# Input-gate block products of a GRU loop in four 32-column groups, spread over all steps

## What is computed

```python
def cell(h, x):
    gi = x @ W_ih + b_ih
    gh = h @ W_hh + b_hh
    i_r, i_z, i_n = jnp.split(gi, 3, axis=-1)
    h_r, h_z, h_n = jnp.split(gh, 3, axis=-1)
    r = jax.nn.sigmoid(i_r + h_r)
    z = jax.nn.sigmoid(i_z + h_z)
    n = jnp.tanh(i_n + r * h_n)
    h_new = (1.0 - z) * n + z * h
    return (h_new, h_new)
```

## Time and profile before

| | us |
|---|---|
| median of three runs | 2352.3 (2351.1 to 2355.22) |
| the profiled execution, its own time | 2354.45 |
| its span, first to last instruction | 2352.6 |
| TensorE matmul busy | 2237.2 (95%) |
| TensorE weight load busy | 1678.7 (71%) |
| VectorE busy | 1406.8 (60%) |
| ScalarE busy | 1184.1 (50%) |
| GpSimd busy | 1141.6 (49%) |
| instructions | 172984 |

### The profile page before, as it was taken

The page is one execution under the profiler, slowest core; times in us unless marked ns, Lnnn a source line. Parts: engine busy times, 40 slices in busy tenths (PEclk is TensorE's granted clock), DMA queues, the critical chain, the costliest instruction groups (busy, mean ns, idle before and its releaser), DMA issues.

```text
span 2352.6 us, 172984 instructions
## 1 busy us (share of the span) xinstructions
PE 2237.2 (95%) x69632; PEld 1678.7 (71%) x69632; DVE 1406.8 (60%) x5056; ACT 1184.1 (50%) x5995; POOL 1141.6 (49%) x3895
## 2 busy tenths in 40 slices
PE   6899999997889999999999999999999999999998
PEld 2223333332369999888999988899998888888887
DVE  1433434343246666677666667766666677777776
ACT  2344444443035555555555555555555555555565
POOL 1142334223125555566555555655555566666665
PEclk8899999998899999999999999999999999999999
DMA  5000000001100000000000000000000000000001
GB/s 232 1 1 1 1 1 1 1 5 50 47 21 15 15 14 8 7 6 7 15 14 17 10 6 5 7 15 14 15 12 6 8 4 7 5 4 7 4 7 71
DMA packets 30281, 40.50 MB, mean 17 GB/s; under 512 B 3296, under 2 KB 24032, under 8 KB 29408
## 3 DMA queue, kind: packets, MB, share of 16 engines
q1 hardware_dynamic: 30032, 36.87, 5.4%
q10 hardware_dynamic: 144, 2.10, 0.2%
HBM read 26.37 MB, written 12.58 MB: 17 GB/s over the span
## 4 chain that ended last, share of the span: by engine, by line
PE 65%; DVE 5%; issue 1%; DMA 0%; ACT 0%; SPq 0%; ACTq 0%
PE ps L1012 57%; PE ps L1038 5%; DVE arena L851 4%; PE ps L1048 3%; DVE arena L868 1%; DMA out<-arena 0%; DMA arena<-gi_d 0%; DVE arena L932 0%; SPq L799 0%; ACT ps L944 0%; SPq L806 0%; ACT arena L997 0%; ACT arena L975 0%; ACT ps L948 0%; ACT arena L980 0%
## 5 line engine op out<-in xcount | busy, mean ns | idle before, releaser
L1012 PE MATMUL ps<-whh,arena 128*4 128x128 f32 (+1 forms) x65536 | 1453.6, 246 | 52.4 <-DVE arena L868 43.6
L1012 PEld LDWEIGHTS ps<-whh,arena 128*4 128x4 f32 x65536 | 1320.0, 87 | 167.9 <-DVE arena L868 84.4
L851 DVE STREAM_TRANSPOSE arena<-ps 128x128 f32<-128x128 f32 x1024 | 432.1, 422 | 260.9 <-PE ps L1012 260.7
L969 ACT ACTIVATE arena<-arena 128x8 f32<-128x8 f32 x1024 | 216.4, 211 | 738.5 <-DVE arena L851 736.8
L1098 POOL TENSOR_TENSOR arena<-tap,seq 128x32 f32<-128x32 f32 x1024 | 231.7, 258 | 368.3 <-DVE seq L881 368.3
L320 DVE TENSOR_REDUCE top<-ps 128x2 f32<-128x1024 f32 x128 | 150.8, 1220 | 281.8 <-PE ps L516 281.8
L868 DVE TENSOR_TENSOR_SCAN arena<-arena 128x24 f32<-128x24 f32 x1024 | 217.2, 212 | 145.5 <-ACT arena L980 145.5
L944 ACT ACTIVATE ps<-arena 128x128 f32<-128x128 f32 x1026 | 269.9, 263 | 3.4 <-DMA arena<-gi_d 3.4
L857 DVE STREAM_TRANSPOSE arena<-ps 128x64 f32<-128x64 f32 x1024 | 256.9, 251 | 16.2 <-PE ps L1012 5.7
L1098 POOL TENSOR_TENSOR arena<-tap,arena 128x32 f32<-128x32 f32 x1024 | 231.6, 257 | 66.8 <-POOL arena L1108 66.8
L170 POOL TENSOR_TENSOR arena<-arena 128x2048 f32<-128x2048 f32 x16 | 72.3, 4520 | 350.0 <-ACT arena L244 350.0
(11 more groups left out here) (94 smaller groups left out, 1573.0 us busy)
## 6 DMA issues: line engine op xcount, KB each, us to landing
arena<-gi_d SPq DMA_DIRECT2D x256, 32.0 KB
gi_d<-arena SPq DMA_DIRECT2D x96, 64.0 KB, 1.6
seq<-in_x SPq DMA_DIRECT2D x4, 1024.0 KB, 16.8
out<-arena SPq DMA_DIRECT2D x16, 256.0 KB, 3.1
whh<-in_w_hh SPq DMA_DIRECT2D x1, 3072.0 KB, 20.1
arena<-in_w_emb ACTq DMA_DIRECT2D x1, 2048.0 KB, 8.2
arena<-in_w_qk SPq DMA_DIRECT2D x4, 512.0 KB, 12.0
arena<-in_w_rz SPq DMA_DIRECT2D x1, 2048.0 KB, 7.6
```

The source lines that it names most:

```text
L851: e.transpose(trn[:, h].rearrange("p q (i c s) -> p q c i s", c=2, s=2)[:, :, :, :, 0], bank[RN[h]][:, 0:P].rearrange("p (q c i) -> p q c ...
L969: e.activation(r_d0[:, h].rearrange("p (i s) -> p i s", s=2)[:, :, 1], trn[:, h, 0, 0:2 * NH].rearrange("p (i s) -> p i s", s=2)[:, :, 0], ...
L1012: last = e.matmul(bank[dst[h]][32 * G:32 * G + B, 0:n], hv, wv[:, k, gates, G, 64 * h:64 * h + 64], start=False, stop=k2 == 1 and k == C - ...
```

## The change

The blocks are made in another form, at other places, and from other loops.

- Form: each 128 x 128 product is made as four products of 32 columns, one to each group of 32 PSUM partitions, as the step's own products are. Blocks alternate between two PSUM banks, 4 and 5.
- Place: the work is cut into chunks of one contraction step (four products: eight matmuls and eight loads). A "turn" is 32 steps and makes the 12 blocks (48 chunks) of one batch and one tile. `spread` deals them out: one chunk in mid step, ahead of the wait for the second half of the state, in 30 of 32 steps, and one more at the end of the step in 18 of 32. Twelve turns make all 144 blocks, over the first 384 steps.
- Operands: the 128 columns of x that a turn needs are first copied into `xb` (two buffers) by a DMA of SyncE's queue.
- Loops: TensorE's code is a loop of 6 iterations whose body has two turns written out, that is 64 steps, and then the old two-step loop for the last 128 steps. VectorE's is three loops of 4 iterations with 32 steps in the body. SyncE's is written out in full. ScalarE's and GpSimd's are as before.

```diff
@@ shared
+        xb = tile([P, 2, C, P])
-        RN, RZ, FB = (0, 1), (2, 3), 4
+        RN, RZ, FB = (0, 1), (2, 3), (4, 5)
+        TURN, NRZ = P // B, 2 * NG
+        BLOCKS = NRZ + C
+        TURNS = (TB - 1) * B
+        def spread():
+            left = [(i, k) for i in range(BLOCKS) for k in range(C)]
+            plan = []
+            for v in range(TURN):
+                mid = [left.pop(0)] if left else []
+                end = [left.pop(0)] if left and (v % 2 == 0 or v % 8 == 7) else []
+                plan.append((mid, end, [i for i, k in mid + end if k == C - 1]))
...
@@ sync
+                def bring_x(m):
+                    src = seq_cb[:, :, m % B, PAD + P * (m // B + 1):PAD + P * (m // B + 2)]
+                    e.dma_start(xb[:, m % 2], src).then_inc(s_xb[m % 2], 16)
...
+                for m in range(TURNS):
+                    for js in (range(0, 2), range(2, 4), range(4, NRZ), range(0)):
+                        for j in js:
+                            keep(m, j)
...
+                        next_half(first)
+                        first += HALF
+                    if m + 2 < TURNS:
+                        e.wait_ge(st["s_block"], BLOCKS * (m + 1))
+                        bring_x(m + 2)
@@ vector
+                for tile_ in range(TB - 1):
+                    with e.Fori(0, B) as b:
+                        m = e.snap(b + B * tile_)
+                        for v, (_, _, whole) in enumerate(plan):
+                            step(b * TURN + (P * tile_ + v), v % 2)
+                            for i in whole:
+                                if i < NRZ:
+                                    take_rz(m, i)
+                                else:
+                                    take_n(m, i, b, P * (tile_ + 1))
@@ tensor
                     e.wait_ge(st["s_seed_rn"], half[1])
                     products(RN, rn, 1, 0)
+                    mid()
                     e.wait_ge(st["s_h"], half[1])
...
                     products(RZ, z, 1, 1).then_inc(st["s_z"], 1)
+                    end()
+                def part(m, par, parts):
+                    for i, k in parts:
+                        if i == 0 and k == 0:
+                            e.wait_ge(s_xb[par], e.snap(m * 8 + (16 - 8 * par)))
+                        if k == 0:
+                            e.wait_ge(st["s_taken"], e.snap(m * BLOCKS + i + 1))
+                        for g in range(NG):
+                            q = slice(32 * g, 32 * g + 32)
+                            if i < NRZ:
+                                w, v = xb[:, par, k, q], wrz[:, k, P * i:P * i + P]
+                            else:
+                                c = i - NRZ
+                                w, v = wn[:, k, P * c + 32 * g:P * c + 32 * g + 32], xb[:, par, k, :]
+                            last = e.matmul(bank[FB[i % 2]][q, 0:P], w, v, start=k == 0, stop=k == C - 1)
+                        if k == C - 1:
+                            last.then_inc(st["s_block"], 1)
...
+                with e.Fori(0, TURNS // 2) as it:
+                    for par in range(2):
+                        m = e.snap(it * 2 + par)
+                        for v, (mid, end, _) in enumerate(plan):
+                            step(m * TURN + v, v % 2, lambda: part(m, par, mid), lambda: part(m, par, end))
+                with e.Fori(0, P // 2) as it:
+                    for v in range(2):
+                        step(it * 2 + (T - P + v), v, lambda: None, lambda: None)
```

More of the change, by code:

```diff
@@ L759, in build @@
         s_kept = [sem("s_kept0"), sem("s_kept1")]
-        RN, RZ, FB = (0, 1), (2, 3), 4
+        s_xb = [sem("s_xb0"), sem("s_xb1")]
+        RN, RZ, FB = (0, 1), (2, 3), (4, 5)
         N_CLEAR = 9
-        TILE_BLOCKS = B * 2 * NG + C * B
+        TURN, NRZ = P // B, 2 * NG
[8 more added lines that the diff above has]
+                plan.append((mid, end, [i for i, k in mid + end if k == C - 1]))
+            assert not left and not plan[-1][2]
+            return plan
+        plan = spread()
         def h_of(u, h):
@@ L812, in _, with keep, next_half @@
             def _(e):
[L813 to L818, removed]
+                def bring_x(m):
+                    src = seq_cb[:, :, m % B, PAD + P * (m // B + 1):PAD + P * (m // B + 2)]
+                    e.dma_start(xb[:, m % 2], src).then_inc(s_xb[m % 2], 16)
+                def keep(m, j):
+                    e.wait_ge(st["s_taken"], 2 + BLOCKS * m + j + 1)
+                    e.dma_start(gi_d[m % B, P * (m // B + 1):P * (m // B + 2), j, :], blk[:, j % 2]).then_inc(s_kept[j % 2], 16)
+                def next_half(first):
+                    e.wait_ge(st["s_seed_z"], 2 * (first - HALF))
+                    load_ring(e, first // HALF % 2, first)
                 for half in range(2):
@@ L823, in _ @@
                     e.sem_inc(s_kept[i], 16)
[L824 to L837, removed]
+                for m in range(2):
+                    bring_x(m)
+                first = 2 * HALF
+                for m in range(TURNS):
+                    for js in (range(0, 2), range(2, 4), range(4, NRZ), range(0)):
+                        for j in js:
+                            keep(m, j)
+                        if first % P == 0:
+                            for i in range(2):
+                                e.wait_ge(s_kept[i], 16 * (1 + (m + 1) * (NRZ // 2)))
+                        next_half(first)
[3 more added lines that the diff above has]
+                        bring_x(m + 2)
+                while first < T:
+                    next_half(first)
+                    first += HALF
                 e.wait_ge(st["s_seed_z"], 2 * T)
@@ L909, in _ @@
                 e.sem_inc(st["s_h"], 2)
[L910 to L931, removed]
+                e.sem_inc(st["s_taken"], 2)
+                for tile_ in range(TB - 1):
[10 more added lines that the diff above has]
+                    for v in range(2):
+                        step(it * 2 + (T - P + v), v)
                 out_copy(e, 1, lambda d, s: e.tensor_copy(d, s))
@@ L1001, in _, with step @@
                 wv = whh[:].rearrange("p c (q G n) -> p c q G n", q=3, G=NG)
-                def step(t, u):
+                def step(t, u, mid, end):
                     half = (e.snap(2 * t + 1), e.snap(2 * t + 2))
```

14 lines of the change are left out of this document (7 added, 7 removed).

## The result

| | before | after |
|---|---|---|
| median of four runs each | 2352.05 us | 2711.27 us (2705.61 to 2714.39) |
| ratio | | 1.1522, 95% interval 1.1498 to 1.1545 |
| span of the profiled execution | 2352.6 us | 2703.8 us |

The change costs 359 us. The forecast was slower, 2930 us, between 2560 and 3150: the sign and the mechanism hold, the size was 219 us too large. In the kernel after, the line of VectorE that runs once per step is L911 (before: L881); the turns are L881 and L887 (L851, L857), the scans L893 and L898 (L863, L868), the products L1035 (L1012), the chunks L1071.

What follows compares the result with a forecast made beforehand. The prediction took fetching TensorE's written-out code as the bound: 432 packets x 4.3 us = 1858 us against 1280 for the first 384 steps, +578, giving a median of 2930 us, range 2560 to 3150.

Steps and rivals of the forecast that it cites:

- What bounds the kernel, and the mechanism: First 384 steps: TensorE's written-out code arrives in 256-instruction packets, one fetched ahead, and their period is the bound.
- The number of packets: TensorE's 64-step body: 71.1 packets, six iterations 427, plus five for returns to its head, 432 in all.
- The period T: TensorE's time from one new code packet to the next in the written-out steps: taken as 4.3 us.
- The sign named for the page: TensorE's code queue q8 would grow from 82 packets to about 490 and 8 MB.
- What speaks for a smaller T: Loops with r/z blocks were entered without any hole, so T was at most about 3.4 to 3.5 us there.
- The returns: TensorE's five jumps back to the head of its 64-step body add one packet each.
- Rival 3: Holes of over 1 us in each packet bring TensorE's clock down to 1.2 GHz: 3318 us, chance 0.03.
- VectorE's returns: Nine jumps to the head of VectorE's 32-step body: between 0 and 9 x 4.4 us, taken as 0.
- The mid chunk: In 30 of 32 steps, eight matmuls among the chain's 96: lengthens the step by 0.22 us.
- The end chunk: In 18 of 32 steps, eight matmuls in TensorE's idle 0.38 us at the step's end: costs nothing.
- The other signs: First 384 steps: TensorE's busy share some 70%, "issue" of 1 to 1.4 us per packet, 400 to 600 us in all.
- The rule of the Trainium skill: The next 16 KiB block is fetched during the present one, crossing mostly hidden: 2315 us without a code cost.

Runs made afterwards that it cites:

- Experiment 1: Kernel before, with TensorE's loop for the last 128 steps given a body of 64 written-out steps instead of 2: 2459.14 us, ratio 1.044.
- experiment 2: Kernel after, with the mid-step chunk moved to the end of its step: 2723.27 us, ratio 1.1567 to the kernel before.
- experiment 3: Kernel before, block products as column groups in short loops with fixed operands: both chunks at the step's end 2303.59 us, one in mid step 2384.26 us.
- experiment 7: Column groups in two-step TensorE bodies, chunks at step's end, operands transferred to fixed addresses, against the kernel before: 2331.96 us, ratio 0.9906.
- experiment 5: Kernel after, with VectorE's loop over the turns written out and TensorE unchanged: 2700.03 us, ratio 1.146 to the kernel before.

## Why the prediction was right, and where it was not

**What bounds the kernel, and the mechanism.** Right. The 384 steps lose time and the last 128 don't; "issue" stands where it was absent; the bound is a packet of 256 instructions. Experiment 1 shows the code alone, experiment 2 that taking the chunk off the chain gains nothing under it, and experiments 3 (both chunks at the end) and 7 that products in this form with kept code are faster than before. That just one packet is fetched ahead fits the times, but no experiment varied it.

**The number of packets.** Right: 432 in the sum, 431 in the trace. The sign named for the page, "from 82 packets to about 490", was a slip of addition: 58 of the 82 belonged to the loops that the change replaces, and 24 + 432 is 456, which is what the page has.

**The period T: the step that failed.** I took 4.3 us, from four pairs in which TensorE visibly stood. The runs have 3.785 on average, 3.73 in the median. 432 x (4.3 - 3.785) = 222 us too much, where the whole miss is 219. The rows were not wrong but chosen: I had timed TensorE from one resumption to the next, and only where a hole was seen, so the slow ones of the kind. I allowed 0.1 us for this (4.40 to 4.3) where 0.6 was due. The trace of before had the answer in another place, the packets' own starts. The earlier trace rows shows one such start. Of the 58 packets after 676 us, 24 start within 5.2 us of the one before them, holes or not (the next longer distance is 8.6 us), and their distances have a mean of 3.78 us and a median of 3.72: the numbers of after. 432 x 3.78 = 1633, +353 on 1280, gives 2705 us, against 2711 measured.

**What speaks for a smaller T.** I read the earlier trace rows as T below 3.5 with TensorE's queue run ahead, and set the lower end by it. That end was the honest one to keep; it held the range.

**The returns.** TensorE's five were given one packet each, 4.3 us. Turns 2, 4, ... 10 with VectorE written out have a first step of 9.0 to 10.5 us against 4.1 on average: some 5.6 us each. In the chain of after at turn 2, 4.13 us are the stop, and at least 1.0 is the clock at its lower level behind it (32 matmuls in 1.89 instead of 1.06 us, a chunk in 0.43 instead of 0.22). Rival 3 had the clock falling in holes of about 1 us throughout; it stayed at 0.99 over the stretch as a whole, and the 0.50 stands behind the long stops shown above. VectorE's returns were taken as 0, since "TensorE's own wait would cover most". That holds for the turns at which TensorE goes back too. At the other six it costs some 3 us each (1.5 in the last); by experiment 5 the sum is 11 us.

**The prices without code.** The mid chunk at 0.22 us on the chain: 3.265 us a step where I had 3.25 (experiment 3). The end chunk at nothing: two of them at the end (0.44 us against a cover of 0.38) cost 0.04 to 0.20 us, 0.12 on average; the 0.20 are in steps followed by a take. The 0.38 us were the idle time of the loads; the matmuls of the same step have 0.19, and the cover measured lies between, at about 0.3. In the kernel after none of this shows.

**The other signs.** TensorE's busy share in the stretch is 80%, not 70%:

```profile
676.00:2305.20 1629.20, 1307.49 (x53760) 1132.94 (x53756) 863.65 (x3602) 689.45 (x4226) 713.90 (x2877) 0.99 0.07 14
```

"Issue" is 12% of 2703.8, 324 us, not 400 to 600. Both follow from T: holes of mostly 0.4 to 1.3 us, 0.7 in the median, where I had 1 to 1.4.

**The rule of the Trainium skill.** The sum by the Trainium skill ("Runtime: NRT & Kernel Launch", section "Instruction fetch mechanics": crossing a block is mostly hidden) was 2315 us. Experiment 1 decides against it for dense matmul code: 0.78 us a step. In the attention stage, where 256 instructions last 29 us, the rows show nothing against it.

## What to carry to other kernels

Count the instructions of a loop's body before writing it out: TensorE code of short matmuls with their loads (11.7 ns an instruction here, 3.03 us for 260) runs at the pace of its packets, 3.7 to 3.8 us for each 256 instructions, unless the body fits in what is kept (6.6 packets did, 8.1 did not), and then a better form of the products is lost in it. Read such a period from the starts of all packets in the queue, not from the holes that happen to be visible. Operands that a short body would need at changing addresses can be brought by a transfer to a fixed place (128 KB a step here), and the waits that this needs belong ahead of the step's last products (18 us here).

## What the runs showed that I had not expected

- A long stop for code leaves TensorE at the lower level of its clock for the next few microseconds: granted 0.50 behind idle times of 4.0 to 5.2 us, 32 matmuls in 1.89 us instead of 1.06. Behind the holes of a packet, 0.7 us in the median, the clock stayed up.
- VectorE stands for its own code as well, 4.64 us at the head of a 32-step body.
- Waits for counts that are worked out in registers cost TensorE time although the transfer that they wait for has landed: 0.2 us for two or three.
- A loop with unchanged text can run 0.17 us slower in every second step when what stands ahead of it changes (experiment 7, last 128 steps). Not explained.
